# Adding the experts' output bias in TensorE's sum instead of in two passes over the tile

## The chip, the cores and the metric

The kernel runs on one core of one Trainium2 chip. The metric is device time in microseconds (us) of one execution, the median of several runs, lower is better. The engines are named as in the profile: PE is TensorE (PEld its weight loads), DVE is VectorE, ACT is ScalarE, POOL is GpSimd, SP is SyncE, which here only issues DMAs.

## The reference

The input is x, 16 sequences of 256 tokens with 128 channels: 4096 tokens. A RWKV block (layer norms, time shift, the wkv recurrence, a squared-ReLU channel mix) is followed by a residual sum and a layer norm. Then comes the part that the change touches, a mixture of 12 experts of which each token uses two:

```python
ys = _geglu(xf @ Ws1 + bs1) @ Ws2 + bs2                  # shared expert
logits = (xf @ Wr + br) / TAU
top_val, top_idx = jax.lax.top_k(logits, 2)
top_w = jax.nn.softmax(top_val, axis=-1)
w = jnp.einsum('nke,nk->ne', jax.nn.one_hot(top_idx, E), top_w)
h = jnp.einsum('nd,edh->enh', xf, We1) + be1[:, None, :]  # 128 -> 2 * 384
act = _geglu(h)
yE = jnp.einsum('enh,ehd->end', act, We2) + be2[:, None, :]
yr = jnp.einsum('end,ne->nd', yE, w)
out = layernorm(x + ys + yr)
```

The bias be2 (12 experts x 128 channels) is added to each expert's result, and the sum is weighed with the token's weight w.

## The kernel before

The first part (up to about 240 us) runs the RWKV block over eight chunks of 512 tokens, each engine following an order of steps that is written out by hand. It also routes: for every token and choice it computes a row in a table in HBM, `dispatched_rows`, in which each expert owns a region. POOL writes the rows there with 64 indirect DMAs (L403). From about 238 us SP places padding rows behind each expert's tokens (L1080, L1081: one register load and one DMA for each of 12 experts). The shared expert's matmuls (L1012, L1018, L1029) end at about 277 us.

The expert part then goes through 75 tiles (`TILES`) of 128 rows, each of one expert. What an engine does for tile n:

- **SP** copies the expert's first weights within SBUF into one of five buffers (`load_weights`, L1095, 384 KB), which waits until the up matmuls of tile n - 5 are done, and then loads the rows of tile n + 5 (`load_rows`, L1088, 68 KB) into one of ten buffers. Each needs a register load first (L1091, L1083). The two are issued in turn, in one queue.
- **PE** multiplies gate and up (`gate_of`, `up_of`, L1250: 3 + 3 matmuls of 128x128 in fp32, each shown as two records), transposes the rows of tile n + 2 (`turn_x`, L1242: one record), and then multiplies the second layer of tile n - 1 into one PSUM bank (`second`, L1268: 3 matmuls, 6 records).
- **ACT** applies Gelu to the gate (`gelu_of`, L1203, 3 operations), copies the transposed rows out of PSUM (`take_x`, L1197), and scales the expert's output bias by each row's weight into `wb` (`weigh_bias`, L1214). `be2_all` holds all 1536 bias values on each of the 128 partitions; SP loads it with one broadcast DMA (L1076), once the buffers that it overlays are free. The expert's number comes from a packed word that ACT loads into a register once for five tiles (`owners_of`).
- **DVE** multiplies up and gate (`act_of`, L1158, 3 operations), and then forms `yo = y * weight + wb` for the tile before (`give_y`, L1166). For every fifth tile it reads where the rows of the next five go (`where_to`, L1143 to L1150), which needs their rows loaded.
- **POOL** scatters `yo` to `routed_rows` in HBM with an indirect DMA (L1126).

Behind the last tile, SP waits for the scatters, loads both contributions back, PE sums them in PSUM, and a layer norm ends the kernel.

`ones_bf` is a 128x128 tile of ones in bf16 that the routing uses already (L387: the ones as stationary operand, in a chain of bf16 matmuls with 12 to 108 columns).

Of the kernel before, what the change touches and what calls it, by code (L numbers as in the profile page):

```python
# [14 lines left out]
def build(nc, x, out, vecs, rows, sqw, wfk, wfv, wrt, ws1, ws2, we1, we2, be1, be2, bs2):  # L15
    F32, BF16 = mybir.dt.float32, mybir.dt.bfloat16
    I32, U32 = mybir.dt.int32, mybir.dt.uint32
    ALU = mybir.AluOpType
# [44 lines left out]
    with ctx:  # L63
# [29 lines left out]
        bs2_col = sb("bs2_col", [P, C // P])  # L93
# [64 lines left out]
        z1 = tmp("z1", [P, CT, C])  # L158
        hT = tmp("hT", [P, SQ, T + 1])
# [7 lines left out]
        nmr3 = tmp("nmr3", [P, CT])  # L167
        pp = tmp("pp", [P, SQ, T + 1])
# [25 lines left out]
        be2_all = sb("be2_all", [P, E * C])  # L194
        after_hT = sb("after_hT", [P, SQ, T + 1])
# [33 lines left out]
        wb = [sb(f"wb{m}", [P, C]) for m in range(2)]  # L229
# [27 lines left out]
        for n in ("bias_spread wb_ready rows_known pads_placed tiles_known tiles_step "  # L257
# [23 lines left out]

        fin = [banks[c][:, :].rearrange("p (n c) -> p n c", c=C) for c in range(CH)]
# [5 lines left out]
        def attention_sync(sp):  # L288
# [15 lines left out]
            sp.dma_start(bs2_col[:, :], bs2.rearrange("(p a) -> p a", a=C // P)).then_inc(s["bias_loaded"], 16)  # L304
# [103 lines left out]
        def attention_vector(v):  # L408
# [57 lines left out]

            def stats(n, tiles, c):
# [120 lines left out]

            done = [0]
# [15 lines left out]
            def shared_take(c):  # L605
                if c == 0:
                    v.wait_ge(s["bias_loaded"], 16)
                v.wait_ge(s2["sh_out"], c + 1)
                at = slice(c * W, (c + 1) * W)
                nv.scalar_tensor_tensor(xnT_all[:, at], sh_y[c][:, :], bs2_col[:, 0:1], xnT_all[:, at], ALU.add, ALU.add).then_inc(s2["sh_taken"], 1)  # L610
# [49 lines left out]
            placed(v, 0, pT[:, PT_PREFIX]); one_over(5); output(5); weigh_v(6); stats2(5)  # L660
# [3 lines left out]
            stats2(7); chosen(v, 2); shared_act(0, 1); x3(6); mix(7); stats3(6)  # L664
# [407 lines left out]
        def experts_sync(sp):  # L1072

            sp.wait_ge(s["hT_psum"], CH)
            sp.wait_ge(s["x0_ready"], CH)
            sp.dma_start(be2_all[:, :], be2.rearrange("e c -> (e c)").partition_broadcast(P)).then_inc(s2["bias_spread"], 16)  # L1076
# [56 lines left out]
        def experts_vector(v):  # L1133
# [27 lines left out]
            def give_y(n):  # L1161
                after2(v, scattered[n % YO], n // YO * 16)
                v.wait_ge(s2["goes_ready"], n // U + 1)
                v.wait_ge(s2["wb_ready"], n + 1)
                v.wait_ge(s2["y_ready"], n + 1)
                nv.scalar_tensor_tensor(yo[n % YO][:, :], ps_y[:, 0:C], goes[n // U % DB][:, n % U, 1:2], wb[n % 2][:, :],  # L1166
                                        ALU.mult, ALU.add).then_inc(s2["yo_ready"], 1)
# [22 lines left out]
        def experts_scalar(a):  # L1190
# [15 lines left out]
            def owners_of(r):  # L1206

                packed_word = a.value_load(packed[0:1, ds(r, 1)])
                return [a.snap((packed_word >> (BITS * (m + 1))) & (2 ** BITS - 1)).with_bounds(min_val=0, max_val=E - 1) for m in range(U)]
# [6 lines left out]
            a.wait_ge(s2["owner_ready"], 1)  # L1216
            take_x(0)
            take_x(1)
            a.wait_ge(s2["bias_spread"], 16)
            for n in range(TILES):  # L1220
                if n % U == 0:
                    e = owners_of(n // U)
                gelu_of(n)
                if n + 2 < TILES:
                    take_x(n + 2)
                weigh_bias(n, e[n % U])
# [9 lines left out]
        def experts_tensor(t):  # L1236
            nt = nc.tensor

# [137 lines left out]
```

## Time and profile before

| | us |
|---|---|
| median of 3 runs | 486.0 |
| lowest and highest | 485.25, 486.16 |
| the profiled execution, whole | 485.25 |
| its span in the trace | 483.5 |

The profiled execution is the fastest of the three. Its span is 1.75 us shorter than its own time; what lies around the span isn't in the trace. Over the span PE is busy 83%, DVE 65%, ACT 62% and POOL 53%, but these are averages over a first part in which the engines take turns at being last, a stretch around 250 us in which PE, DVE and ACT stand nearly still, and the expert part from 277 to 452 us, which is 36% of the span. A time in a row is us from the start of the span, a mean is in ns.

### The profile page before, as it was taken

How to read it: one execution, taken by the hardware profiler on the slowest of the kernel's cores; microseconds unless marked ns; L12 is line 12 of the kernel's file. 1: busy time of each engine (PE TensorE's matmuls, PEld its weight loads, DVE VectorE, ACT ScalarE, POOL GpSimd, SP SyncE). 2: the span in 40 equal slices, each digit the busy share in tenths (PEclk: the TensorE clock that was granted, in tenths of full speed). 3: DMA queues.
4: the chain of work that ended last, by engine and by line, in shares of the span. 5: the costliest groups of instructions: out<-in, count | busy, mean ns of one | idle time of the engine just before them, and what ended most of it. 6: DMA issues, size and time to landing. Idle time of an engine off the chain costs nothing.

```text
span 483.5 us, 10004 instructions
## 1 busy us (share of the span) xinstructions
PE 403.4 (83%) x2503; PEld 307.7 (64%) x2503; DVE 314.1 (65%) x1065; ACT 297.9 (62%) x715; POOL 256.9 (53%) x328
## 2 busy tenths in 40 slices
PE   0276898998987979989464999999999999999992
PEld 0134456756746556664221489999999999999840
DVE  4769899999997996734521446665555655555252
ACT  2476699989785956754101167776666766666145
POOL 3657657567478867877472014444433443444264
PEclk9997899999999998999795989999999999999997
DMA  5399600000002001011121546766666666665294
GB/s 148 87 206 385 186 1 0 2 1 1 2 12 105 32 12 42 32 44 47 40 76 47 192 141 232 246 233 225 242 237 223 224 229 242 228 221 198 82 335 127
DMA packets 51471, 64.86 MB, mean 134 GB/s; under 512 B 8924, under 2 KB 35292, under 8 KB 51416
## 3 DMA queue, kind: packets, MB, share of 16 engines
q1 hardware_dynamic: 46968, 54.85, 34.3%
q0 software_dynamic: 4448, 9.38, 5.9%
q8 instruction: 22, 0.36, 0.3%
q14 instruction: 33, 0.27, 0.2%
HBM read 21.65 MB, written 13.91 MB: 74 GB/s over the span
## 4 chain that ended last, share of the span: by engine, by line
PE 46%; DVE 21%; issue 12%; SPq 8%; DMA 3%; POOL 3%; ACT 3%; another core or an unknown queue 2%; DVEq 0%; ACTq 0%; POOLq 0%
PE bank L1250 18%; PE bank L1268 9%; PE bank L981 4%; PE bank L963 3%; DVE bst L471 2%; SPq L1081 2%; DVE rec L551 2%; POOL frs L816 2%; SPq L1080 2%; PE bank L1018 1%; SPq L1095 1%; PE bank L1242 1%; PE bank L993 1%; DVE pp L507 1%
## 5 line engine op out<-in xcount | busy, mean ns | idle before, releaser
L1126 POOL DMA_INDIRECT routed_rows<-yo,goes_to x75 | 72.0, 959 | 123.8 <-DVE yo L1166 120.9
L1250 PE MATMUL bank<-xT,w 128*128 128x128 f32 x900 | 117.3, 280 | 3.5 <-issue 1.2
L1250 PEld LDWEIGHTS bank<-xT,w 128*128 128x128 f32 x900 | 108.9, 194 | 6.2 <-issue 3.6
L1158 DVE SCALAR_TENSOR_TENSOR actT<-bank,tile_bias,gl 128x128 f32<-128x128 f32 x225 | 65.6, 345 | 26.3 <-ACT gl L1203 13.2
L1203 ACT ACTIVATE gl<-bank,tile_bias 128x128 f32<-128x128 f32 x225 | 66.5, 365 | 24.2 <-PE bank L1250 23.5
L403 POOL DMA_INDIRECT dispatched_rows<-rows_all,slot_i x64 | 64.2, 1003 | 23.5 <-issue 17.3
L1268 PE MATMUL bank<-we_sb,actT 128*128 x450 | 63.8, 278 | 1.6 <-DVE yo L1166 1.1
L1268 PEld LDWEIGHTS bank<-we_sb,actT 128*128 128x128 f32 x450 | 56.1, 191 | 4.0 <-issue 3.6
L1166 DVE SCALAR_TENSOR_TENSOR yo<-bank,goes,wb 128x128 f32<-128x128 f32 x75 | 26.2, 350 | 34.2 <-PE bank L1268 28.2
L1197 ACT ACTIVATE xT<-bank 128x128 f32<-128x128 f32 x75 | 20.8, 278 | 32.2 <-PE bank L1242 22.9
L963 PE MATMUL bank<-xk,wfk_sb 128*128 128x512 f32 x64 | 32.5, 617 | 4.1 <-DVE xk L568 3.0
L602 DVE SCALAR_TENSOR_TENSOR below_m<-bank,v_sb,below_p 128x512 f32<-128x512 f32 x16 | 12.0, 748 | 36.0 <-remote 20.4
L914 PE MATMUL bank<-hT,mixa 128*128 128x512 f32 x48 | 28.6, 681 | 6.9 <-ACT hT L714 6.1
L776 ACT ACTIVATE below_p<-bank,v_sb 128x512 f32<-128x512 f32 x16 | 11.0, 687 | 37.7 <-remote 17.5
L981 PEld LDWEIGHTS bank<-wfv_sb,kf 128*128 128x128 f32 x256 | 29.4, 192 | 3.6 <-ACT kf L771 2.9
L981 PE MATMUL bank<-wfv_sb,kf 128*128 128x128 f32 x256 | 30.4, 277 | 0.8 <-ACT kf L771 0.8
L1214 ACT ACTIVATE wb<-be_all,goes 128x128 f32 x75 | 30.1, 402 | 1.2 <-issue 0.8
L900 PE MATMUL bank<-ident,z 128*128 128x128 f32 x64 | 10.6, 291 | 22.8 <-ACT z L685 22.8
L844 POOL TENSOR_TENSOR rstd<-veps,half 128x4 f32<-128x4 f32 x24 | 27.8, 1156 | 1.9
L1029 PE MATMUL bank<-below_m,ws_sb 128*128 128x512 f32 x32 | 19.1, 727 | 9.9 <-DVE below_m L602 9.8
L551 DVE RECIPROCAL rec<-nd 128x512 f32<-128x512 f32 x8 | 26.7, 3341 | 0.1
L915 PE MATMUL bank<-hT,mixb 128*128 128x512 f32 x48 | 26.7, 640 | 0.0
(201 smaller groups left out, 772.8 us busy)
## 6 DMA issues: line engine op xcount, KB each, us to landing
w<-we_sb SPq DMA_DIRECT2D x75, 384.0 KB
x_all<-dispatched_rows SPq DMA_DIRECT2D x75, 68.0 KB
we_sb<-we SPq DMA_DIRECT2D x1, 4608.0 KB
rows_all<-x SPq DMA_DIRECT2D x8, 256.0 KB, 2.7
x_all<-routed_rows SPq DMA_DIRECT2D x8, 256.0 KB, 4.9
rows_all<-routed_rows SPq DMA_DIRECT2D x8, 256.0 KB, 5.1
out<-x_all SPq DMA_DIRECT2D x8, 256.0 KB, 2.5
routed_rows<-yo,goes_to POOLq DMA_INDIRECT x75
```

What stands on the lines that cost most here:

```text
L403: ng.indirect_dma_start(dispatch, bass.IndirectOffsetOnAxis(ap=slot_i[:, k, n:n + 1], axis=0), rows_all[:, n, :], None).then_inc(s["dispat ...
L551: nv.reciprocal(rec[:, :], nd[:, 1, :]).then_inc(s["rec_ready"], 1)
L844: ng.tensor_tensor(rstd[n][:, :], veps[n][:, :], half[:, :], ALU.pow).then_inc(s["pow" + n], 1)
L914: nt.matmul(o, mixa[:, n, :], hT[:, :, 1:T + 1], start=True, stop=False)
L963: nt.matmul(pf[j % 2][:, :], wfk_sb[:, j * P:(j + 1) * P], xk2[:, :], start=True, stop=True).then_inc(s["fk_ready"], 1)
L981: last = nt.matmul(pkv[:, n * P:(n + 1) * P], kf[:, j, n * P:(n + 1) * P], wfv_sb[:, j, :], start=j == 0, stop=j == HF - 1)
L1126: ng.indirect_dma_start(routed, bass.IndirectOffsetOnAxis(ap=goes_to[n // U % DB][:, n % U:n % U + 1], axis=0), yo[n % YO][:, :], None).th ...
L1158: nv.scalar_tensor_tensor(actT[n % UA][:, at], ps_a[j][:, 0:P], tile_bias[:, j, n:n + 1], gl[n % 2][:, at], ALU.add, ALU.mult).then_inc(s2 ...
L1203: na.activation(gl[n % 2][:, j * P:(j + 1) * P], ps_g[j][:, 0:P], ACT.Gelu, bias=tile_bias[:, HK + j, n:n + 1]).then_inc(s2["gelu_ready"], 1)
L1214: na.activation(wb[n % 2][:, :], be2_all[:, ds(e * C, C)], ACT.Copy, scale=goes[n // U % DB][:, n % U, 1:2]).then_inc(s2["wb_ready"], 1)
L1250: return nt.matmul(to[:, 0:P], w1[m][:, off:off + P], xT[m][:, :], start=True, stop=True)
L1268: last = nt.matmul(ps_y[:, 0:C], actT[m][:, j * P:(j + 1) * P], we2_sb[:, ds(e, 1), j, :].rearrange("p a c -> p (a c)"), start=j == 0, sto ...
```

## The change

The bias is no longer scaled by ACT and added by DVE. PE adds it while the tile's second layer is still being summed in PSUM, so that DVE only multiplies by the weight: `(y + b) * w` in place of `y * w + b * w`.

For this the bias is split into three bf16 parts whose sum is the fp32 value (`split_biases`, five small DVE operations on 128x13 elements, placed behind `output(5)`). The parts are moved by three small DMAs into partitions 0, 1 and 2 of a new tile `bias_rows` (bf16, 128 x 1536), whose other partitions are zero (`zero_bias_rows`, a memset placed ahead of `stats2(7)`). A matmul with `ones_bf` as stationary operand sums the partitions and so puts the bias on every row of the tile (`biased`).

What goes: ACT's operation, its register load and its waits; the wait of DVE on `wb_ready`; the broadcast DMA of 768 KB and SP's waits ahead of it. What comes: one bf16 matmul for each tile, the five operations and the memset on DVE, one more small load and the three DMAs on SP, and a wait of PE for these ahead of the tiles. The buffers `z1` and `hT` change places with some small ones, so that `bias_rows` overlays `z0` and `z0w`.

```diff
+        braw = sb("braw", [P, NB])
+        bpart = [sb(f"bpart{n}", [P, NB], BF16) for n in range(3)]
...
-        be2_all = sb("be2_all", [P, E * C])
-        after_hT = sb("after_hT", [P, SQ, T + 1])
+        bias_rows = sb("bias_rows", [P, E * C], BF16)
...
-            sp.dma_start(bs2_col[:, :], bs2.rearrange("(p a) -> p a", a=C // P)).then_inc(s["bias_loaded"], 16)
+            sp.dma_start(braw[:, 0:B2], be2.rearrange("e h -> (e h)").rearrange("(p a) -> p a", a=B2)).then_inc(s["bias_loaded"], 16)
+            sp.dma_start(braw[:, B2:NB], bs2.rearrange("(p a) -> p a", a=NB - B2)).then_inc(s["bias_loaded"], 16)
...
+            def split_biases():
+                v.wait_ge(s["bias_loaded"], 2 * 16)
+                for n, (of, to) in enumerate(((braw, bleft), (bleft, bleft2))):
+                    nv.tensor_copy(bpart[n][:, :], of[:, :]).then_inc(s["split"], 1)
+                    v.wait_ge(s["split"], 2 * n + 1)
+                    nv.tensor_tensor(to[:, :], of[:, :], bpart[n][:, :], ALU.subtract).then_inc(s["split"], 1)
+                    v.wait_ge(s["split"], 2 * n + 2)
+                nv.tensor_copy(bpart[2][:, :], bleft2[:, :]).then_inc(s["split"], 1)
...
+            def zero_bias_rows():
+                nv.memset(bias_rows[:, :], 0.0).then_inc(s["rows_zero"], 1)
...
-            placed(v, 0, pT[:, PT_PREFIX]); one_over(5); output(5); weigh_v(6); stats2(5)
+            placed(v, 0, pT[:, PT_PREFIX]); one_over(5); output(5); split_biases(); weigh_v(6); stats2(5)
...
-            stats2(7); chosen(v, 2); shared_act(0, 1); x3(6); mix(7); stats3(6)
+            zero_bias_rows(); stats2(7); chosen(v, 2); shared_act(0, 1); x3(6); mix(7); stats3(6)
...
-            sp.wait_ge(s["hT_psum"], CH)
-            sp.wait_ge(s["x0_ready"], CH)
-            sp.dma_start(be2_all[:, :], be2.rearrange("e c -> (e c)").partition_broadcast(P)).then_inc(s2["bias_spread"], 16)
+            sp.wait_ge(s["rows_zero"], 1)
+            sp.wait_ge(s["split"], 5)
+            for n in range(3):
+                sp.dma_start(bias_rows[n:n + 1, :], bpart[n][:, 0:B2]).then_inc(s2["rows_moved"], 16)
...
-                v.wait_ge(s2["wb_ready"], n + 1)
                 v.wait_ge(s2["y_ready"], n + 1)
-                nv.scalar_tensor_tensor(yo[n % YO][:, :], ps_y[:, 0:C], goes[n // U % DB][:, n % U, 1:2], wb[n % 2][:, :],
-                                        ALU.mult, ALU.add).then_inc(s2["yo_ready"], 1)
+                nv.tensor_scalar(yo[n % YO][:, :], ps_y[:, 0:C], goes[n // U % DB][:, n % U, 1:2], None, ALU.mult).then_inc(s2["yo_ready"], 1)
...
-            def weigh_bias(n, e):
-                a.wait_ge(s2["goes_ready"], n // U + 1)
-                after2(a, "yo_ready", n - 1)
-                na.activation(wb[n % 2][:, :], be2_all[:, ds(e * C, C)], ACT.Copy, scale=goes[n // U % DB][:, n % U, 1:2]).then_inc(s2["wb_ready"], 1)
...
+            def biased(to, row, width):
+
+                return nt.matmul(to, ones_bf[:, :], bias_rows[:, ds(row, width)], start=False, stop=True)
...
-                    last = nt.matmul(ps_y[:, 0:C], actT[m][:, j * P:(j + 1) * P],
-                              we2_sb[:, ds(e, 1), j, :].rearrange("p a c -> p (a c)"), start=j == 0, stop=j == HK - 1)
-                last.then_inc(s2["y_ready"], 1)
+                    nt.matmul(ps_y[:, 0:C], actT[m][:, j * P:(j + 1) * P],
+                              we2_sb[:, ds(e, 1), j, :].rearrange("p a c -> p (a c)"), start=j == 0, stop=False)
+                biased(ps_y[:, 0:C], e * C, C).then_inc(s2["y_ready"], 1)
...
+            t.wait_ge(s2["rows_moved"], 3 * 16)
```

How the instructions stand in a row is shown at two places. First PE in the middle of the expert part, from the last up matmul of one tile to the first gate matmul of the next (bank6 is the last up bank, bank7 the bank of the second layer, bank0 the first of the gate). Before:

```order
L1250 MATMUL bank6<-xT2,w1_2 128x128 [waits e_act_ready]
L1242 MATMUL bank4<-ident,x0_all 128x128 [waits e_xT_ready,x_loaded2_9]
L1268 REGISTER_ALU [waits e_yo_ready,e_act_ready]
...
L1268 ISA
L1268 MATMUL bank7<-we2_sb,actT1 128x128
L1250 MATMUL bank0<-xT3,w1_3 128x128 [waits e_gelu_ready,w1_loaded3,e_xT_ready]
```

And with the change:

```order
L1255 MATMUL bank6<-xT2,w1_2 128x128 [waits e_act_ready]
L1247 MATMUL bank4<-ident,x0_all 128x128 [waits e_xT_ready,x_loaded2_9]
L1273 REGISTER_ALU [waits e_yo_ready,e_act_ready]
...
L1273 ISA
L1273 MATMUL bank7<-we2_sb,actT1 128x128
L1242 ISA
L1242 MATMUL bank7<-bias_rows,ones_bf 128x128
L1255 MATMUL bank0<-xT3,w1_3 128x128 [waits e_gelu_ready,w1_loaded3,e_xT_ready]
```

The bf16 matmul and one register instruction stand between the last fp32 matmul of the second layer and the next gate.

The second place is ACT at the start of the expert part (gl is the Gelu's result, xT the transposed rows). Before:

```order
L1197 ACTIVATE xT0<-bank4 128x128 [waits e_xT_psum,e_owner_ready,e_bias_ready]
L1197 ACTIVATE xT1<-bank4 128x128 [waits e_xT_psum]
L1208 TENSOR_LOAD packed [waits e_bias_spread]
L1203 ACTIVATE gl0<-bank0,tile_bias 128x128 [waits e_gate_ready]
...
L1197 ACTIVATE xT2<-bank4 128x128 [waits e_xT_psum]
L1214 REGISTER_ALU [waits e_goes_ready]
...
L1214 ACTIVATE wb0<-be2_all,goes0 128x128
L1203 ACTIVATE gl1<-bank0,tile_bias 128x128 [waits e_gate_ready]
```

With the change:

```order
L1213 ACTIVATE xT0<-bank4 128x128 [waits e_xT_psum,e_bias_ready]
L1213 ACTIVATE xT1<-bank4 128x128 [waits e_xT_psum]
L1219 ACTIVATE gl0<-bank0,tile_bias 128x128 [waits e_gate_ready]
...
L1213 ACTIVATE xT2<-bank4 128x128 [waits e_xT_psum]
L1219 ACTIVATE gl1<-bank0,tile_bias 128x128 [waits e_gate_ready]
```

The register load, two register instructions, the move of an address and the scaling are gone between the copy of one tile's rows and the Gelu of the next tile.

## Rows read from the trace of the kernel before

**Rows 1.** Busy time by stretch: us, then PE, PEld, DVE, ACT, POOL, PEclk, DMA share, GB/s.

```profile
277.00:452.00 175.00, 168.18 (x1425) 162.87 (x1426) 99.99 (x360) 116.55 (x375) 70.93 (x74) 0.99 0.63 217
```

**Rows 2.** Page, part 5: groups of instructions of the expert part.

```profile
L1250 PE MATMUL bank<-xT,w 128*128 128x128 f32 x900 | 117.3, 280 | 3.5 <-issue 1.2
...
L1166 DVE SCALAR_TENSOR_TENSOR yo<-bank,goes,wb 128x128 f32<-128x128 f32 x75 | 26.2, 350 | 34.2 <-PE bank L1268 28.2
...
L1214 ACT ACTIVATE wb<-be_all,goes 128x128 f32 x75 | 30.1, 402 | 1.2 <-issue 0.8
```

**Rows 3.** Timeline of PE: start us, us, engine line operation; transpositions mark the tiles.

```profile
284.15 0.27 PE L1242 MATMUL bank<-ident,x_all 128*128 128x128 f32 x1
...
291.28 1.57 PE L1250 MATMUL bank<-xT,w 128*128 128x128 f32 x12
...
373.33 0.27 PE L1242 MATMUL bank<-ident,x_all 128*128 128x128 f32 x1
...
375.45 0.27 PE L1242 MATMUL bank<-ident,x_all 128*128 128x128 f32 x1
...
439.57 1.58 PE L1250 MATMUL bank<-xT,w 128*128 128x128 f32 x12
...
445.22 0.27 PE L1242 MATMUL bank<-ident,x_all 128*128 128x128 f32 x1
```

**Rows 4.** Timeline of SP's queue: weight copies of tiles 5, 20 and 70, and a row load.

```profile
284.66 0.50 SPq L1095 DMA_DIRECT2D w<-we_sb  x1
...
318.83 0.49 SPq L1095 DMA_DIRECT2D w<-we_sb  x1
319.90 0.34 SPq L1088 DMA_DIRECT2D x_all<-dispatched_rows  x1
...
434.93 0.49 SPq L1095 DMA_DIRECT2D w<-we_sb  x1
```

**Rows 5.** Chain that ended last, 374 to 396 us: start us, us, what.

```profile
373.93 0.49 SPq L1095
...
376.14 0.49 SPq L1095
...
377.21 0.71 SPq L1088
...
387.89 4.16 DMA w<-we_sb
...
392.14 1.58 PE bank L1250 x12
```

**Rows 6.** Timeline of POOL in the same stretch.

```profile
377.17 0.96 POOL L1126 DMA_INDIRECT routed_rows<-yo,goes_to  x1 [1.16 <-DVE yo L1166]
```

**Rows 7.** Timelines of PE and PEld: fp32 matmuls with 12 columns, and bf16 ones.

```profile
214.79 1.05 PE L951 MATMUL bank<-wrt_sb,xnT_all 128*128 128x12 f32 x8 [1.50 <-issue]
...
227.52 1.02 PE L1012 MATMUL bank<-xnT_all,ws_sb 128*128 128x512 f32 x2
...
228.43 0.39 PE L387 MATMUL bank<-sel,ones_bf 128*128 128x96 bf16 x8
228.67 1.11 PE L1018 MATMUL bank<-xnT_all,ws_sb 128*128 128x512 f32 x2
...
228.38 0.34 PEld L387 LDWEIGHTS bank<-sel,ones_bf 128*128 128x128 bf16 x8 [0.18 <-issue]
```

**Rows 8.** Timeline of DVE where its new operations go, and two small operations.

```profile
149.11 0.87 DVE L471 BATCH_NORM_STATS2 bst<-x1c 128x6 f32<-128x128 f32 x4 [2.51 <-ACT x1c L751]
...
192.59 0.87 DVE L471 BATCH_NORM_STATS2 bst<-x1c 128x6 f32<-128x128 f32 x4 [4.08 <-ACT x1c L751]
...
238.73 0.17 DVE L620 TENSOR_TENSOR ntl<-run_f,base_tile 128x12 f32<-128x12 f32 x1
238.94 0.18 DVE L621 TENSOR_TENSOR_SCAN edge_of<-ones_ex,ntl 128x13 f32<-128x13 f32 x1
```

**Rows 9.** Waits of SP's queue: us in total, times, longest.

```profile
SPq L1080 <- DVE wait_here L617: 88.3, 1, 88.3
```

More of the change, by code:

```diff
@@ L92, in build @@
         LN1W, LN1B, LN2W, LN2B, DECAY, FIRST, TMK, TMV, TMR, CMK, CMR, BS1 = range(12)
-        bs2_col = sb("bs2_col", [P, C // P])
+        NB = (E * C + C) // P
+        braw = sb("braw", [P, NB])
+        bleft = sb("bleft", [P, NB])
+        bleft2 = sb("bleft2", [P, NB])
+        bpart = [sb(f"bpart{n}", [P, NB], BF16) for n in range(3)]
+        B2 = E * C // P
         be1_sb = sb("be1_sb", [E, H1])
@@ L157, in build @@
         z0w = tmp("z0w", [P, CT, C])
-        z1 = tmp("z1", [P, CT, C])
-        hT = tmp("hT", [P, SQ, T + 1])
         bst = {n: tmp(f"bst{n}", [P, CT, 6]) for n in "0123"}
@@ L167, in build @@
         nmr3 = tmp("nmr3", [P, CT])
+        z1 = tmp("z1", [P, CT, C])
+        hT = tmp("hT", [P, SQ, T + 1])
         pp = tmp("pp", [P, SQ, T + 1])
@@ L228, in build @@
         yo = [sb(f"yo{m}", [P, C]) for m in range(YO)]
-        wb = [sb(f"wb{m}", [P, C]) for m in range(2)]
         w1 = [sb(f"w1_{m}", [P, H1]) for m in range(U)]
@@ L256, in build @@
         s2 = {}
-        for n in ("bias_spread wb_ready rows_known pads_placed tiles_known tiles_step "
+        for n in ("rows_moved rows_known pads_placed tiles_known tiles_step "
                   "word_psum code_psum code_ready bias_psum bias_ready owner_ready own_ready goes_step goes_ready "
@@ L280, in gate_bank @@
             return pkv if j and c >= EARLY else pv
+        bs2_col = braw[:, B2:NB]
         fin = [banks[c][:, :].rearrange("p (n c) -> p n c", c=C) for c in range(CH)]
@@ L606, in shared_take @@
                 if c == 0:
-                    v.wait_ge(s["bias_loaded"], 16)
+                    v.wait_ge(s["bias_loaded"], 2 * 16)
                 v.wait_ge(s2["sh_out"], c + 1)
                 at = slice(c * W, (c + 1) * W)
-                nv.scalar_tensor_tensor(xnT_all[:, at], sh_y[c][:, :], bs2_col[:, 0:1], xnT_all[:, at], ALU.add, ALU.add).then_inc(s2["sh_taken"], 1)
+                nv.scalar_tensor_tensor(xnT_all[:, at], sh_y[c][:, :], bs2_col, xnT_all[:, at], ALU.add, ALU.add).then_inc(s2["sh_taken"], 1)
             def find_tiles():
@@ L1204, in gelu_of @@
                                   bias=tile_bias[:, HK + j, n:n + 1]).then_inc(s2["gelu_ready"], 1)
-            def owners_of(r):
-                packed_word = a.value_load(packed[0:1, ds(r, 1)])
-                return [a.snap((packed_word >> (BITS * (m + 1))) & (2 ** BITS - 1)).with_bounds(min_val=0, max_val=E - 1) for m in range(U)]
-            def weigh_bias(n, e):
-                a.wait_ge(s2["goes_ready"], n // U + 1)
-                after2(a, "yo_ready", n - 1)
-                na.activation(wb[n % 2][:, :], be2_all[:, ds(e * C, C)], ACT.Copy, scale=goes[n // U % DB][:, n % U, 1:2]).then_inc(s2["wb_ready"], 1)
-            a.wait_ge(s2["owner_ready"], 1)
             take_x(0)
             take_x(1)
-            a.wait_ge(s2["bias_spread"], 16)
             for n in range(TILES):
-                if n % U == 0:
-                    e = owners_of(n // U)
                 gelu_of(n)
@@ L1225, in experts_scalar @@
                     take_x(n + 2)
-                weigh_bias(n, e[n % U])
             for c in range(CH):
```

## The prediction

> **What bounds the kernel now.** I read the windows first, to see which part the change touches: the expert part, 277 to 452 us, in which PE is busy 168.2 of 175.0 us at a granted clock of 0.99, ACT 116.6 and DVE 100.0 [rows 1]. That looks like a PE bound. The timeline of PE says how tight it is. In a tile without a stall one transposition follows the last after 2.12 us (373.33 to 375.45) [rows 3], and a tile is 12 records of gate and up (900 over 75 tiles) [rows 2], 6 of the second layer and the transposition: 19 records, so 0.1116 us each. From the transposition at 284.15 to that at 445.22 there are 71 tiles in 161.07 us [rows 3], where 71 x 2.12 would be 150.5. So 10.5 us of the part are stalls, and something else than PE limits it as well.
>
> That something is SP's queue. Its weight copies for tiles 5 and 20 are issued 34.17 us apart, 2.278 each, and those for tiles 20 and 70 116.1 us apart, 2.322 each; over all 65 it is 2.312 [rows 4]. In the chain of waits SP's instructions follow one another without a wait: from copy to copy 2.21 us in the best case (373.93 to 376.14) [rows 5]. It is slower than a clean PE tile, so PE eats up its lead. The copy of tile 5 is issued 6.62 us ahead of its matmuls (284.66, 291.28), that of tile 70 only 4.64 us (434.93, 439.57) [rows 3, 4]; and it can't be much less, since a copy takes 4.16 us to land and the gate starts 0.09 us behind it (387.89, 392.14) [rows 5]. The lead of 6.62 - 4.25 = 2.37 us is used up after 2.37 / (2.278 - 2.12) = 15 tiles, about tile 20. From there PE waits for SP.
>
> **The change, part by part.**
>
> *The bf16 matmul, 75 times.* What a record costs here is the load of its weights, not its columns: eight fp32 records with 12 columns take 1.05 us [rows 7], of which the last one's own duration is some 0.28 [rows 2], so (1.05 - 0.28) / 7 = 0.110 us each, as much as with 128 columns. A bf16 load is short: eight in 0.34 us, at most 0.043 each [rows 7]. But the next fp32 load begins only when the bf16 matmul starts and can't hide behind an fp32 matmul any more: the two fp32 matmuls behind a bf16 one span 1.11 us where two behind an fp32 one span 1.02 [rows 7], 0.09 more. So a bf16 matmul ahead of an fp32 load costs nearly one full record. Bounds: 0.05 us (0.39 / 8, the bf16 matmuls with up to 96 columns [rows 7]) and 0.112 (a record). I take 0.107, nearest to the 0.09 and the 0.112. PE's tile becomes 2.227 us and its sum grows by 75 x 0.107 = 8.0 us. The register instruction ahead of it runs in the sequencer, as the three of the fp32 matmuls do in tiles without a stall: nothing.
>
> The Trainium skill, "TensorE: Matmul & The Clock Gate", section "Back-to-back issue gap", gives about 81 ns for a sustained pair of load and matmul with 128 columns; by it the sum would be 6.1 us. Its section "LDWEIGHTS (loading the stationary operand)" gives columns / 1.2, so 107 ns for 128, which agrees with the 0.112 here.
>
> *What ACT loses.* 75 x 0.402 = 30.1 us of work [rows 2], with a register load in every fifth tile. ACT is busy 116.6 of 175 us and doesn't bound a tile [rows 1]: nothing.
>
> *What DVE loses.* The wait for `wb`; the multiplication stays, of 0.350 us, and waited mostly for PE's second layer (28.2 of 34.2 us) [rows 2]. Between 0 and the rest that wasn't PE's, 6 us; DVE too is far from full [rows 1], so 0.
>
> *The end of the expert part.* It is the later of two times for the start of tile 70's matmuls, 439.57 before [rows 3].
> - By PE: it starts tile 5 at 291.28, later by the four bf16 matmuls until then, 0.43. Without stalls tile 70 starts at 291.71 + 65 x 2.227 = 436.5.
> - By SP: the copy of tile 5 goes out at 284.66, unchanged. Copy 70 follows 65 intervals later, and the matmuls 4.64 us behind it. At 2.278, the rate of the stretch in which PE doesn't stall: 284.66 + 148.1 + 4.64 = 437.4. At 2.322, the rate of the later stretch: 440.2. At 2.21, the best case: 432.9, so PE decides.
>
> Which rate? SP is slowed where POOL's indirect DMA, 0.96 us from 377.17, falls on SP's row DMA: that took 0.71 us from 377.21, where one took 0.34 away from it [rows 4 to 6]. PE's tile sets POOL's beat. In the late stretch, where PE waits for SP, both beats lock with POOL's on top of SP's. A PE at 2.227 is as slow as an SP at about 2.26 and stays out of this longer, as in the first 15 intervals. So I take 2.278 and 437.4, 2.2 us ahead of 439.57. Behind it come six bf16 matmuls (those of tiles 69 to 74), 0.64. Sum: -1.5 us, with bounds -2.5 (PE decides: 436.5 - 439.57 + 0.64) and +1.3 (2.322). At the low price of 0.05 PE's own end only moves ahead, and SP's stays: the price hardly matters.
>
> *The first part.* The five small operations on DVE: one follows the other after 0.21 us [rows 8], 1.05 us together. They go ahead of the states of chunk 6, behind which DVE waits 2.51 us for ACT [rows 8]: hidden; without that cover +1.05. The memset goes where DVE waits 4.08 us for ACT [rows 8], hidden; no row has its size, and I bound it by a 128x512 operation, 0.87 us [rows 8]. SP's three small DMAs wait for that memset, at about 190 us, and stand ahead of the padding, for which SP sits waiting 88.3 us [rows 9]: nothing, or 3 x 0.5 us if they came late. The broadcast that goes was issued into the same wait: between 0 and -0.5.
>
> **The sum.** 485.25 - 1.5 = 483.7 for an execution like the profiled one. The median of the runs lies 0.75 above it: **484.5**.
>
> **The rivals.**
> - *SP keeps its whole mean of 2.312.* Its end for tile 70 is then that of before, and only the six last matmuls are added: +0.6, 486.6. For it: 50 of 65 intervals ran at 2.322 [rows 4]. Against: they ran in the lock that a slower PE avoids.
> - *The stalls aren't SP's but belong to the group of five tiles.* DVE reads where rows go for each five, and PE waits behind DVE. If such a stall has a fixed size, a slower PE doesn't absorb it, and the price comes in full: 75 x 0.107 = +8.0, 494. It decides if the leads of copies at the stalls are well above 4.25 us. Against: at tile 70 the lead is 4.64, and the first 15 tiles hardly stall though they have the same groups. In between, half of the stalls being fixed gives about +3, 489.
> - *The first part moves.* The five operations or SP's DMAs aren't hidden: up to +1.05 and +1.5, 487 to 488 if the end stays.
> - *PE decides alone* (SP at 2.26 or less): -2.5, 483.5; with less at the start and a cheaper bf16 matmul, 482.5.
>
> **How the numbers follow.** 0.2% is 1 us, about what a measurement of this kernel can tell from no change. My forecast with the PE-bound case beside it: 45%. SP as before, or the forecast with a small loss in the first part: 30%. Fixed stalls in full 12%, in part or a loss in the first part 13%. Faster 0.45, same 0.30, slower 0.25. The forecast's own range is 482.7 to 485.6. The range that should hold 8 in 10 reaches to 490 and leaves out the full price (12%) and some 6% below 482.3.
>
> **What would show it.** In the profile of the changed kernel a tile without a stall should take 2.23 us (2.17 if the bf16 matmul costs only its columns). The bf16 group should have 75 records, and the gate behind each start 0.11 us later. From the fourth transposition to the last, 71 tiles should take 159 to 161 us and the stalls 1 to 3 us in place of 10.5. Copies 5 and 70 should be 148 us apart (150.3 before). ACT should lose 30 us of busy time. The first row load and the first tile should stand where they do, within 1 us. I'm wrong if SP's intervals stay at 2.31, if stalls stay at 10 us beside longer tiles, or if the expert part starts later.

## The result, and the profile after

The changed kernel takes 488.75 us (median of 13 runs, 486.58 to 492.09), the kernel before 486.0 in the same rounds. The medians are 2.75 us apart, where I had forecast 1.5 us faster. The ratio is 1.0082, 95% interval 1.0059 to 1.0104, which is 4.0 us and more than the medians say: it is that of the means of all 38 executions of the changed kernel on record (489.64) and of the 13 of the kernel before (485.62). So the loss here is 2.75 to 4.0 us. Of all executions below, one is left out of the numbers: one of e16's six, which took 1410.45 us. The profiled execution of the changed kernel took 491.54 us, with a span of 489.8; before it was 485.25 and 483.5. So the two profiled executions are 6.3 us apart where the medians are 2.75 apart, and a difference between these two traces alone isn't the price of the change. I come back to that below with more executions.

Busy time of the expert part, 4 us later than in [rows 1] since everything begins later (columns as there), and what the page groups there, to be held against [rows 2]:

```profile
281.00:456.00 175.00, 171.88 (x1492) 168.05 (x1493) 98.91 (x358) 87.67 (x300) 70.10 (x73) 0.98 0.62 216
```

```profile
L1255 PE MATMUL bank<-xT,w 128*128 128x128 f32 x900 | 119.5, 283 | 1.4 <-DVE actT L1176 0.5
...
L1183 DVE TENSOR_SCALAR yo<-bank,goes 128x128 f32<-128x128 f32 x75 | 26.3, 350 | 38.9 <-PE bank L1242 36.5
```

ACT has gone from 116.6 to 87.7 us: its scaling is away, nearly the 30.1 us that it had. DVE's `give_y` still takes 350 ns and still waits, now for the bf16 matmul (L1242). PE is fuller, 171.9 of 175 for 168.2. The view of line L1242 alone shows the new work, one line for each kind of instruction with its shortest, middle and longest duration in ns:

```profile
L1242 PEldq FUSED_REGOPS  x75: 46/46/46, 288.0 to 457.4; - x75
L1242 PEld LDWEIGHTS bank<-bias_rows,ones_bf x75: 100/100/100, 289.3 to 457.8; 128*128 128x128 bf16 x75
L1242 PE MATMUL bank<-bias_rows,ones_bf x75: 219/219/219, 289.4 to 457.9; 128*128 x75
```

The durations overlap with their neighbours, so the price is read from starts. PE's timeline, answering to [rows 3]:

```profile
288.62 0.27 PE L1247 MATMUL bank<-ident,x_all 128*128 128x128 f32 x1
290.85 0.27 PE L1247 MATMUL bank<-ident,x_all 128*128 128x128 f32 x1
...
295.31 0.27 PE L1247 MATMUL bank<-ident,x_all 128*128 128x128 f32 x1
295.42 0.83 PE L1273 MATMUL bank<-we_sb,actT 128*128 x6
296.09 0.22 PE L1242 MATMUL bank<-bias_rows,ones_bf 128*128 x1
296.14 1.56 PE L1255 MATMUL bank<-xT,w 128*128 128x128 f32 x12
297.54 0.27 PE L1247 MATMUL bank<-ident,x_all 128*128 128x128 f32 x1
...
450.99 0.27 PE L1247 MATMUL bank<-ident,x_all 128*128 128x128 f32 x1
```

A tile without a stall takes 2.23 us (288.62 to 290.85, 295.31 to 297.54) where it took 2.12: the bf16 matmul costs 0.11 (0.109 with three digits, 2.228 less 2.119), though the next gate starts only 0.05 behind it. From the fourth transposition to the last there are 71 tiles in 162.37 us, 161.07 before. The longer tiles make 71 x 0.11 = 7.8 us of that; the stalls fell from 10.5 to 4.0. SP's queue, answering to [rows 4] (the copies of tiles 5, 20 and 70; the last row holds two copies):

```profile
288.77 0.52 SPq L1113 DMA_DIRECT2D w<-we_sb  x1
...
323.81 0.49 SPq L1113 DMA_DIRECT2D w<-we_sb  x1
...
440.38 1.50 SPq L1113 DMA_DIRECT2D w<-we_sb  x2
```

151.61 us for the 65 intervals, 2.332 each, where it was 2.312. The chain of waits runs through SP as it did in [rows 5], one instruction behind the other from copy to copy (L1109 and L1101 are the register loads):

```profile
291.01 0.49 SPq L1113
291.54 0.27 SPq L1101
291.89 0.07 SPq L1106
292.08 0.34 SPq L1106
292.46 0.52 SPq L1109
293.20 0.49 SPq L1113
```

Of these 2.19 us, 0.83 are the two DMA issues (0.49 and 0.34), and 0.79 are the two register loads (0.27 and 0.52).

In the first part the new operations stand where they were put. DVE's timeline at the two places of [rows 8], and SP's waits, where [rows 9] had one of 88.3 us:

```profile
146.23 0.17 DVE L475 CAST bpart<-braw 128x13 bf16<-128x13 f32 x1
146.44 0.17 DVE L477 TENSOR_TENSOR bleft<-braw,bpart 128x13 f32<-128x13 f32 x1
...
150.09 0.87 DVE L485 BATCH_NORM_STATS2 bst<-x1c 128x6 f32<-128x128 f32 x4 [1.56 <-ACT x1c L768]
...
190.88 0.70 DVE L604 MEMSET bias_rows<- 128x768 uint32 x1
194.65 0.88 DVE L485 BATCH_NORM_STATS2 bst<-x1c 128x6 f32<-128x128 f32 x4 [3.07 <-ACT x1c L768]
```

```profile
SPq L1098 <- DVE wait_here L634: 48.6, 1, 48.6
SPq L1094 <- DVE bias_rows L604: 44.3, 1, 44.3
```

The five operations follow each other after 0.21 us, as estimated, and the wait behind them is 1.56 for 2.51 us; the memset takes 0.70 and the wait is 3.07 for 4.08. The covers took both. On SP the memset now holds the three small DMAs until it is done, 44.3 us, which fell into the wait that was there before. Yet the first transposition of the expert part starts at 281.84, where it was 277.88: 4 us that no new instruction accounts for. The chain of waits has pieces that it gives to no engine and no known queue. In the kernel before, from 226 to 236 us:

```profile
228.66 2.88 another core or an unknown queue
...
231.71 3.36 another core or an unknown queue
```

and in the changed one, from 205 to 235 us:

```profile
213.13 5.92 another core or an unknown queue
...
230.59 2.33 another core or an unknown queue
```

### The profile page after: what moved, and what is told of

Read it like the earlier page. It is cut to its first block, busy times and chain, and to the rows that moved or that the text cites. A ratio compares the mean times of both kernels' runs of the same rounds, so it can differ in the third digit from the quotient of the medians.

```text
span 489.8 us, 9786 instructions
## 1 busy us (share of the span) xinstructions
PE 409.8 (84%) x2578; PEld 315.6 (64%) x2578; DVE 314.8 (64%) x1071; ACT 268.6 (55%) x640; POOL 256.4 (52%) x328
## 4 chain that ended last, share of the span: by engine, by line
PE 34%; SPq 22%; DVE 16%; issue 13%; ACT 5%; DMA 3%; POOL 3%; another core or an unknown queue 2%; ACTq 0%; DVEq 0%; POOLq 0%
PE bank L1255 9%; SPq L1113 6%; SPq L1106 5%; PE bank L1273 4%; SPq L1109 4%; PE bank L980 4%; PE bank L998 3%; SPq L1101 3%; SPq L1098 2%; SPq L1099 2%; PE bank L931 2%; DVE bst L485 2%; PE bank L932 2%; PE bank L1010 1%
## 5 line engine op out<-in xcount | busy, mean ns | idle before, releaser
L1255 PE MATMUL bank<-xT,w 128*128 128x128 f32 x900 | 119.5, 283 | 1.4 <-DVE actT L1176 0.5
L1183 DVE TENSOR_SCALAR yo<-bank,goes 128x128 f32<-128x128 f32 x75 | 26.3, 350 | 38.9 <-PE bank L1242 36.5
L980 PE MATMUL bank<-xk,wfk_sb 128*128 128x512 f32 x64 | 35.0, 657 | 4.7 <-DVE xk L582 3.0
L931 PE MATMUL bank<-hT,mixa 128*128 128x512 f32 x48 | 27.4, 654 | 8.3 <-ACT hT L731 7.5
L998 PE MATMUL bank<-wfv_sb,kf 128*128 128x128 f32 x256 | 30.1, 276 | 0.5 <-ACT kf L788 0.5
L1247 PE MATMUL bank<-ident,x_all 128*128 128x128 f32 x75 | 21.0, 280 | 7.8 <-DMA x_all<-dispatched_rows 7.8
L917 PEld LDWEIGHTS bank<-ident,z 128*128 128x128 f32 x64 | 8.2, 154 | 29.4 <-issue 23.6
```

The source lines that it names most:

```text
L931: nt.matmul(o, mixa[:, n, :], hT[:, :, 1:T + 1], start=True, stop=False)
L980: nt.matmul(pf[j % 2][:, :], wfk_sb[:, j * P:(j + 1) * P], xk2[:, :], start=True, stop=True).then_inc(s["fk_ready"], 1)
L998: last = nt.matmul(pkv[:, n * P:(n + 1) * P], kf[:, j, n * P:(n + 1) * P], wfv_sb[:, j, :], start=j == 0, stop=j == HF - 1)
L1255: return nt.matmul(to[:, 0:P], w1[m][:, off:off + P], xT[m][:, :], start=True, stop=True)
```

## The experiments

18 kernels ran, in five groups, each group on one chip, each kernel in five rounds against the kernel before. In three of these groups (e1 to e4, e9 to e12, e17 and e18) the kernel before takes 462 us, in the two others (e5 to e8, e13 to e16) 487. I call them the groups at 462 and at 487; the two profiles above, of 485.25 and 491.54 us, are of the kind at 487. What makes the difference isn't known, and that it is the chip isn't shown: the record gives the same chip number, 10, for e13 to e16 (487) and for e17 and e18 (462).

The difference lies ahead of the expert part. In the groups at 462 the first transposition stands near 255 us and the chain of waits has no piece of unknown origin. The largest single part of it is SP's placing of the padding rows. It takes 29.3 to 30.5 us in every profile at 487, and 15.1 to 15.6 in every one at 462, with and without the change. First the kernel before (487), then e12 (462), the same twelve DMAs (shortest, middle and longest in ns, first and last start in us):

```profile
L1081 SPq DMA_DIRECT2D dispatched_rows<-pad_rows x12: 5/510/725, 239.4 to 268.9; - x12
```

```profile
L1083 SPq DMA_DIRECT2D dispatched_rows<-pad_rows x12: 496/516/657, 229.3 to 244.1; - x12
```

The expert part takes nearly the same time in both kinds (about 1 us more at 487). So a kernel is compared only with the kernel before in its own group.

For each kernel I give the ratio with its 95% interval, and from its profile "71 tiles" (fourth to last transposition) with the stalls in them (what they take beyond the clean tile's time), and SP's mean interval from copy 5 to copy 70.

### Is it the matmul, or what was taken away? (e1 to e3)

**e1**: the kernel before without the weighed bias. be2 is left out of the result here, and in e2, e11, e14, e17 and e18.

```diff
-            sp.dma_start(be2_all[:, :], be2.rearrange("e c -> (e c)").partition_broadcast(P)).then_inc(s2["bias_spread"], 16)
...
-                nv.scalar_tensor_tensor(yo[n % YO][:, :], ps_y[:, 0:C], goes[n // U % DB][:, n % U, 1:2], wb[n % 2][:, :],
-                                        ALU.mult, ALU.add).then_inc(s2["yo_ready"], 1)
+                nv.tensor_scalar(yo[n % YO][:, :], ps_y[:, 0:C], goes[n // U % DB][:, n % U, 1:2], None, ALU.mult).then_inc(s2["yo_ready"], 1)
...
-                weigh_bias(n, e[n % U])
```

> The kernel before without the weighed bias: ACT's operation, its register loads, DVE's wait and the broadcast DMA of 768 KB are gone, and be2 is left out of the result. Theory A (SP's queue limits the expert part; what the change takes from ACT and DVE is worth nothing): no change, -0.5 to +0.5 us against before. Rival (ACT's relief is worth something): -2 us or more, all of it in the expert part.

Measured: 462.51 for 462.15 us, 1.0005 (0.9993 to 1.0017). 71 tiles 161.45, stalls 10.9, SP 2.314. Taking 30 us of work from ACT and a wait from DVE gives nothing.

**e2**: the change without its matmul.

```diff
-                    nt.matmul(ps_y[:, 0:C], actT[m][:, j * P:(j + 1) * P],
-                              we2_sb[:, ds(e, 1), j, :].rearrange("p a c -> p (a c)"), start=j == 0, stop=False)
-                biased(ps_y[:, 0:C], e * C, C).then_inc(s2["y_ready"], 1)
+                    last = nt.matmul(ps_y[:, 0:C], actT[m][:, j * P:(j + 1) * P],
+                              we2_sb[:, ds(e, 1), j, :].rearrange("p a c -> p (a c)"), start=j == 0, stop=j == HK - 1)
+                last.then_inc(s2["y_ready"], 1)
```

> The changed kernel without the bf16 matmul (be2 is left out of the result): it differs from e1_no_wb by the additions in the first part alone (five small DVE operations, the memset, one small load, three small DMAs of SP, the order of buffers). Theory A (the loss sits ahead of the expert part and comes from these additions): +2.5 to +4 us against before, the first expert tile 3 to 4 us later. Rival B (the first part's waits for an unknown queue only vary from run to run; the loss is the bf16 matmul's): -0.5 to +1 us against before.

Measured: 462.24 us, 0.9997 (0.998 to 1.0013). 71 tiles 159.99, stalls 9.5, SP 2.300. Without the matmul nothing of the loss is left in this group, so the first part isn't it here.

**e3**: the kernel before with a bf16 matmul of zeros behind each second layer.

```diff
+            nv.memset(zero_bf[:, :], 0.0)
...
-                last.then_inc(s2["y_ready"], 1)
+                nt.matmul(ps_y[:, 0:C], ones_bf[:, :], zero_bf[:, :], start=False, stop=True).then_inc(s2["y_ready"], 1)
```

> The kernel before with one more bf16 matmul for each tile (ones by a tile of zeros, into the same sum; nothing else is changed). Theory A (SP's queue limits the part, so a longer PE tile is mostly hidden): +0.5 to +1.5 us, a tile without a stall 2.23 us in place of 2.12. Rival (the price is seen in full): +8 us. Rival B (the whole loss is the matmul's): +4 us.

Measured: 464.64 us, 1.0053 (1.0034 to 1.0073): +2.5. 71 tiles 160.92, stalls 2.6, SP 2.294. The matmul alone makes a loss of this size, with ACT's and DVE's old work still in place. It is more than my theory's +0.5 to +1.5 and less than the rival's +4.

### Is SP's queue the limit? (e4, e16)

**e4** and **e16**: the kernel before, where SP keeps the expert's number of tile n in a register from its row load to its weight copy, instead of loading the word a second time. The DMAs and their order are the same.

```diff
             def load_rows(n):
                 at = sp.value_load(word[0:1, n:n + 1])
+                if n >= U:
+                    owner_kept[n] = sp.snap(at & 15).with_bounds(min_val=0, max_val=E - 1)
...
             def load_weights(n):
-                at = sp.value_load(word[0:1, n:n + 1])
-                e = sp.snap(at & 15).with_bounds(min_val=0, max_val=E - 1)
+                e = owner_kept.pop(n) if n >= U else sp.snap(sp.value_load(word[0:1, n:n + 1]) & 15).with_bounds(min_val=0, max_val=E - 1)
```

> The kernel before with one register load less for each tile on SP: the word of tile n, read for its rows, is kept for its weight copy. Theory A (SP's instructions, 2.31 us for each tile, limit the expert part): SP's interval falls to about 1.95 us where it isn't held, PE's tiles run at 2.12 without stalls, the 71 tiles take 151 us in place of 161, and the time falls by 8 to 10 us. Rival (the stalls come from the DMAs' landing times or from DVE's work for each five tiles): no change within 1 us.

> The kernel of e4 (before with one register load less for each tile on SP): -9 to -11 us on any chip, 71 tiles in 150.5 to 151 us, since PE's tile and SP's interval are the same on the chips seen.

Measured: e4 452.17 for 462.15 us, 0.9772 (0.9754 to 0.9791); e16, in a group at 486.83, 477.65, 0.981 (0.9775 to 0.9846), so -9.2 us. The windows of e4 over its expert part, columns as in [rows 1]:

```profile
261.00:411.00 150.00, 150.00 (x1346) 149.99 (x1345) 93.76 (x339) 110.38 (x355) 66.80 (x70) 1.00 0.70 247
```

PE has no idle time at all. 71 tiles take 150.64 us, which is 71 x 2.12, and the stalls are 0.1 us. e16's profile has 151.39 us, so 0.9 of stalls, a little more than expected. SP's copies follow each other as PE frees the buffers:

```profile
329.91 0.49 SPq L1098 DMA_DIRECT2D w<-we_sb  x1
331.05 0.34 SPq L1092 DMA_DIRECT2D x_all<-dispatched_rows  x1
332.03 0.49 SPq L1098 DMA_DIRECT2D w<-we_sb  x1
```

One register load less in each of 70 tiles takes 10 us off in e4 and 9.2 in e16. That shows that SP's queue limits the kernel before, and that its 10.5 us of stalls are SP's. At the start of the part, where SP is still ahead of PE's buffers, its first three intervals are 1.64 to 1.68 us in e4, where the same queue needed 2.21 at best with both loads. It is also a version that beats both kernels, without the change.

### What does the matmul cost where nothing covers it? (e7, e8)

**e7**: the change with e4's edit. **e8**: e3 (the matmul of zeros) with e4's edit. **e5** and **e6** are the changed kernel and the kernel before once more, in the same group (486.73 us).

> The changed kernel, unaltered, beside the kernel before on the chip of this call. e3 showed that the matmul alone costs 2.5 us, and e1 and e2 that all the rest of the change costs nothing on their chip. Theory A' (the loss is the matmul's, and the first part of the change is free): +2 to +3 us. Rival (the first part of the change costs on top): +4 us or more.

> The kernel before, unaltered, as if it were another: no change, within 0.5 us. Its profile gives the start of the expert part and the 71 tiles for this chip: 71 tiles in 160.5 to 161.5 us.

> The changed kernel with one register load less for each tile on SP. Theory A (with SP out of the way PE decides, and the bf16 matmul is seen in full): 71 tiles in 158.3 us (2.23 each, no stalls), so 3 us less than before, and 8 us more than the kernel before with the same edit (e4: 150.6 us for the 71 tiles). Rival (the matmul costs what it cost in e3, 2.5 us, whatever limits the part): 71 tiles in 153 us.

> The kernel before with one register load less on SP and with the bf16 matmul of zeros, nothing else changed. Theory A: as e7_after_one_load within 1 us, so about 2 us faster than before, since the rest of the change (relief of ACT and DVE, first part) is worth nothing. Rival (ACT's relief counts once PE decides): slower than e7 by 2 us or more.

| | us | ratio | 71 tiles | stalls | SP |
|---|---|---|---|---|---|
| e5 | 489.26 | 1.0049 (1.0022 to 1.0075) | 161.92 | 3.6 | 2.335 |
| e6 | 486.44 | 1.0012 (0.9989 to 1.0035) | 159.94 | 9.4 | 2.306 |
| e7 | 487.11 | 1.0006 (0.9981 to 1.0031) | 158.84 | 0.5 | 2.206 |
| e8 | 485.93 | 0.999 (0.9966 to 1.0014) | 158.75 | 0.4 | 2.204 |

PE's timeline of e7, two transpositions near the start of the part and the last two:

```profile
285.78 0.27 PE L1250 MATMUL bank<-ident,x_all 128*128 128x128 f32 x1
288.00 0.27 PE L1250 MATMUL bank<-ident,x_all 128*128 128x128 f32 x1
...
440.17 0.27 PE L1250 MATMUL bank<-ident,x_all 128*128 128x128 f32 x1
442.39 0.27 PE L1250 MATMUL bank<-ident,x_all 128*128 128x128 f32 x1
```

With SP out of the way PE alone sets the pace in both: 158.8 against the 150.6 of e4, 8.2 us for 71 matmuls, 0.115 each (0.105 against e16, which is of a group at 487 as e7 is). This is the price in full, and here it eats the whole gain of e4: e7 and e8 stand where the kernel before stands. In the changed kernel as it is, SP's slowness hides most of it.

The tiles came out as expected, the times didn't: I had expected 3 us less for e7 and 2 less for e8, and the medians are at +0.4 and -0.8. From the first transposition to the end of the span e7 and e8 take 203.5 and 203.8 us, 2.1 to 2.4 less than e6 (205.9). By that 1.3 to 2.8 us are lost ahead of the tiles in the timed executions, and where is open. The profiles can't tell: that of e7 is an execution of 482.52 us, 4.6 below its own median. e6's 71 tiles are 0.6 us under what I expected too.

### What is left of it in the kernel as it is? (e9 to e12)

In one group at 462.03 us: **e9** the changed kernel, **e10** e3 again, **e11** e2 again, and **e12** the kernel before with 75 bf16 matmuls behind PE's last sum, where no one waits for them. e12 asks whether a longer program of PE costs something by itself.

```diff
+            t.wait_ge(s2["fin_out"], 1)
+            for n in range(TILES):
+                nt.matmul(banks[0][:, 0:C], ones_bf[:, :], zero_bf[:, :], start=True, stop=True)
```

> The changed kernel unaltered, as the measure for the three beside it on this chip. From e5: +2 to +4 us against before. In the profile 71 tiles in 161 to 162.5 us, 1 to 2 more than before.

> The kernel of e3 (before with the bf16 matmul of zeros alone) beside the changed one on the same chip. Theory A' (the whole loss is the matmul's): as e9 within 0.7 us. Rival C (the additions in the first part cost 1 to 2 us where the chip is slow, as e7 against e8 hints): 1 to 2 us less than e9.

> The kernel of e2 (the change without its matmul, be2 left out) on this chip. Theory A': within 0.7 us of before, as in e2. Rival C: +1 to +2 us.

> The kernel before with 75 bf16 matmuls of zeros placed behind PE's last sum, where PE has nothing to do until the end, so that its program is as long as with the change and no tile is. Rival D (a longer program of PE costs time in the first part, through instruction fetches): +1 to +2 us. Theory A' (the loss is the tiles' own): within 0.5 us of before.

| | us | ratio | 71 tiles | stalls | SP |
|---|---|---|---|---|---|
| e9 | 464.43 | 1.0043 (1.0026 to 1.006) | 160.18 | 1.8 | 2.308 |
| e10 | 463.96 | 1.0039 (1.0019 to 1.0059) | 160.47 | 2.1 | 2.304 |
| e11 | 462.4 | 1.0013 (0.9998 to 1.0028) | 159.58 | 9.1 | 2.302 |
| e12 | 461.74 | 0.9991 (0.9976 to 1.0006) | 159.09 | 8.6 | 2.294 |

The matmul is again the loss (+1.9 alone, +2.4 with everything), and not by the length of the program as such: e12 has as many, placed behind the tiles, and costs nothing. e9's 71 tiles are under the 161 to 162.5 that I expected. e12's last row of PE also gives the price of bf16 matmuls in a row. The row's 4.35 us hold the last one's own 0.22, so they start (4.35 - 0.22) / 74 = 0.056 us apart, half of what one costs between fp32 matmuls:

```profile
450.36 4.35 PE L1318 MATMUL bank<-zero_bf,ones_bf 128*128 128x128 bf16 x75
```

### Does the first part cost something of its own? (e13 to e15, e17, e18)

In a group at 486.83 us: **e13** the changed kernel, **e14** without the matmul (as e2), **e15** the matmul of zeros alone (as e3). Then, to tell a cost of the additions from scatter between programs, **e17** (as e1) and **e18** (as e2) in one group.

> The changed kernel unaltered, as the measure for e14 and e15: +2 to +4 us against before.

> The kernel of e2 (the change without its matmul, be2 left out). Theory A' (the first part of the change is free): within 0.7 us of before on any chip. Rival C (it costs where the chip is slow): +1 to +2 us if the kernel before takes 486 us here.

> The kernel of e3 (before with the matmul of zeros alone). Theory A': as e13 within 0.7 us. Rival C: 1 to 2 us less than e13 if the kernel before takes 486 us here.

> The kernel before without the weighed bias, as e1: ACT's scaling, its register loads, the wait of DVE and the broadcast are gone, nothing is added (be2 is left out of the result). Theory: the additions of the change to the first part cost something on a chip where the kernel before takes 486 us, and the removals nothing: ratio within 0.998 and 1.002, no different from the kernel before. Rival: the scatter between programs on such a chip is itself 0.5%, so that any changed program can stand at 1.005 to 1.006 there: then this kernel too may lie outside 0.998 to 1.002. On a chip where the kernel before takes 462 us both expect 0.999 to 1.001.

> The change without its matmul, as e2, e11 and e14 (be2 is left out of the result): the split, the memset, the three DMAs and the new places of the buffers stay. Theory, that these cost 2.8 us on a chip where the kernel before takes 486 us: ratio 1.004 to 1.008 there, and 1.000 to 1.001 on a chip where it takes 462 us. Rival, that the 2.8 us of e14 were scatter: ratio within 0.998 and 1.003 on the former too.

| | us | before | ratio | 71 tiles | stalls | SP |
|---|---|---|---|---|---|---|
| e13 | 489.22 | 486.83 | 1.0068 (1.0042 to 1.0094) | 162.38 | 4.0 | 2.328 |
| e14 | 489.6 | 486.83 | 1.0062 (1.003 to 1.0094) | 160.97 | 10.4 | 2.299 |
| e15 | 488.55 | 486.83 | 1.0034 (1.0006 to 1.0063) | 160.89 | 2.6 | 2.303 |
| e17 | 463.13 | 462.1 | 1.0008 (0.9991 to 1.0026) | 159.16 | 8.6 | 2.290 |
| e18 | 461.71 | 462.1 | 0.9999 (0.9987 to 1.0012) | 159.27 | 8.7 | 2.278 |

e14 is at +2.8 us with no matmul in it, which neither the theory (0.7 at most) nor the rival (1 to 2) allowed. That speaks for a cost of the first part in a group at 487. But it doesn't add up with the others: the matmul alone gives +1.7 (e15), and both together (e13) give +2.4, no more than e14 by itself. In the pair e7 and e8, which differ by the first part and by ACT's and DVE's relief, it is 1.2 us. e17 and e18 came to a group at 462, where e18 repeats e2: nothing. They so left the question open for which they were made. In such groups the first part costs -0.4 to 0.5 us (e18, e2, e11, e9 less e10), and in those at 487 between 0.7 (e13 less e15) and 2.8 (e14), which isn't settled.

One difference between the two kinds bears on it. At 462 the chain to the first transposition runs through POOL's row DMAs, the last of which ends at 249.4 to 251.4 us, when SP has long placed the padding (243.3 to 245.7). At 487 it is the other way round: POOL's end at 258.1 to 263.7 and the padding at 268.8 to 275.4, and the chain runs through the padding, which starts when DVE has the row numbers. So a delay of DVE there has no cover behind it at 487. That this is what e14 shows is argued, not shown.

Nor is it known what makes the waits of unknown origin: they are 8.1 us in the chain of the kernel before (four pieces), 12.3 in that of e6 (three), 10.9 in that of the changed kernel (three), and in the groups at 462 there are none in the chain. They come without the change too, at other places each time, so it is not shown that the change adds to them.

## Why the prediction was wrong, point by point

All profiles together, to take some of the scatter out: nine profiles without the matmul (the kernel before, e1, e2, e6, e11, e12, e14, e17, e18), seven with it (the changed kernel, e3, e5, e9, e10, e13, e15).

| means, us | without | with |
|---|---|---|
| 71 tiles | 160.1 (159.1 to 161.5) | 161.3 (160.2 to 162.4) |
| stalls in them | 9.5 | 3.0 |
| SP's interval, copy 5 to 70 | 2.300 | 2.315 |
| from the issue of copy 70 to the last transposition | 10.3 | 10.8 |
| first transposition to the end of the span | 205.2 | 206.9 |

Most of the profiles with the whole change are of groups at 487, and most of those without the matmul of groups at 462, so two of these rows are also given apart (number of profiles in brackets):

| means, us | without | matmul alone | whole change |
|---|---|---|---|
| SP's interval, groups at 487 | 2.306 (3) | 2.303 (1) | 2.332 (3) |
| SP's interval, groups at 462 | 2.296 (6) | 2.299 (2) | 2.308 (1) |
| first transposition to the end, at 487 | 205.9 | 206.4 | 207.7 |
| first transposition to the end, at 462 | 204.8 | 206.2 | 206.0 |

- **The price of the bf16 matmul** was right: 0.107 taken, 0.11 measured in a clean tile, 0.105 to 0.115 in e7 against e16 and e4. The reason that I gave, that the fp32 load behind it can't be hidden, agrees with e12, where bf16 matmuls in a row cost 0.056, but no run tests it by itself. One reading in it was wrong: a bf16 load isn't 0.043 us short. The eight loads of [rows 7] take 96 to 99 ns each and overlap, so that 0.043 says only how closely they follow each other. In the changed kernel the load takes 100 ns. The Trainium skill, "TensorE: Matmul & The Clock Gate", section "LDWEIGHTS (loading the stationary operand)", gives columns / 1.2, so 107 ns for 128 columns. The trace's 100 ns is near that. For a sustained pair of load and matmul with 128 columns the Trainium skill, on the same page, section "Back-to-back issue gap", gives about 81 ns. Neither number here agrees with it: one bf16 matmul between fp32 ones costs 0.109 us, and e12's 75 pairs in a row 0.056 each.
- **SP's queue as the limit** was right, and is shown by e4 and e16.
- **The relief of ACT and DVE at nothing** was right (e1, e17).
- **The absorption by stalls** was right in kind and nearly in size. I forecast 159 to 161 us for the 71 tiles and 1 to 3 us of stalls; the profile of the changed kernel has 162.4 and 4.0, the mean of the seven is 161.3 and 3.0. Of 7.8 us, 6.5 vanish in the stalls.
- **The step that failed is SP's rate.** I took 2.278, that of the first 15 intervals, for the whole part, and so -2.2 us for the matmuls of tile 70. I explained the 2.322 of the later ones by POOL's DMAs falling in step with SP's, out of which a slower PE would keep. The profiles don't show such an effect. With the matmul SP's mean is 2.294 to 2.335, and never lower than the lowest without (2.278). Nor does it matter whether POOL's DMA falls on SP's row DMA: in e12 the 47 intervals in which it does take 2.290 us in the mean, the 18 others 2.306; in the kernel before it is 2.331 and 2.261, but in the changed one 2.336 and 2.326. And the early stretch isn't a quicker one: over the nine profiles without the matmul the first 15 intervals are at 2.299 and the other 50 at 2.300, in e12 at 2.311 and 2.289. About four intervals in five are ordinary ones, 2.264 us in the kernel before and 2.268 in the changed one, and the others are long, 12 of mean 2.52 and 13 of mean 2.59. The kernel before had two of them in its first 15, as few as any of the nine, and I had built a mechanism on it. They aren't mere chance either, though POOL's beat isn't their reason: the intervals behind copies 23 and 37 are long (over 2.40 us) in all 16 profiles and that behind copy 51 in 14, so at these three the place in SP's program counts. What happens there is open. At SP's unchanged mean the term is 0 in place of -2.2.
- **The six last matmuls** (+0.64) were right: from the issue of copy 70 to the last transposition the time grows by 0.5.
- **What is then left** is my first rival, "SP keeps its whole mean", with +0.6, 486.6. Measured is more, by the medians +2.4 to +2.75 for the whole change in its four groups (by the ratios +2.0 to +4.0), and +1.7 to +2.5 for the matmul alone. Only a part of the rest can be placed. At 487 the whole change makes SP's interval longer, by 0.026 in the mean, 65 x 0.026 = 1.7 us; the matmul alone doesn't there (2.303), and at 462 the one profile of the whole change (2.308) lies within those without (2.278 to 2.314). Why the whole change slows SP at 487 is open. From the first transposition to the end of the span, which holds both SP's term and the last six matmuls, the whole change adds 1.8 us at 487 and 1.2 at 462, the matmul alone 0.5 and 1.4. What is lost ahead of the first transposition the profiles can't size: it stands at 277.3 to 283.8 us in the groups at 487 and at 254.4 to 256.4 in those at 462, with and without the first part of the change.
- **The first part**: the covers for the five operations, the memset and SP's DMAs held as worked out, and in the groups at 462 its cost was within what I allowed. That the first tile stands 4 us later in the profile after can be the scatter of single executions in large part: at 487 the five profiles with the first part have it at 280.4 in the mean (277.3 to 282.2), the five without at 279.5 (277.9 to 283.8). The rest is open, see e14.
- **Fixed stalls, in full**: refuted. In e4 the stalls are gone, so none were fixed.

The range held 488.75; the sign and the chances didn't. The mistake behind them is that I took a gain of 2.2 us from a difference of 0.044 us between two stretches of one execution, and gave the case without it only 30%. A matmul added to the engine next to the limit had no row that showed a gain from it; its sure terms were zero or positive, but for the broadcast's 0 to -0.5.

## What to carry to other kernels

Where one queue issues two DMAs for each tile, count its register loads too: here they were a third of its interval, and one of them less was worth 9 to 10 us, where 30 us taken from a busy engine off the path were worth nothing. Work that is added to the second slowest engine is hidden up to the limit's pace, but the start and the end of the pipeline still pay, and once the limit is lifted the full price comes back. A rate read from 15 intervals of one execution isn't a mechanism: see first whether a second execution has it. And a trace of one group stands only for its own kind: two means that mix groups at 462 and at 487 in different shares differ by that alone.

## What the runs showed of the hardware

- A bf16 matmul of 128 columns costs 0.11 us between fp32 ones (2.12 to 2.23 us for a clean tile) and 0.056 in a row of its kind (e12).
- A register load by SP takes 0.27 and 0.52 us in the chain of the changed kernel. To drop one in each tile brought SP's mean interval from 2.31 to 2.10 us (e4), where PE's pace was the limit; where it wasn't, from 2.21 to 1.64 to 1.68.
- The same kernel takes 462 us in some groups and 487 in others. The clean tile is 2.12 us in both. Ahead of the expert part the twelve padding DMAs of SP take 30 us in place of 15, and ACT and DVE wait for something that the profile has no name for. The mean granted clock of the profiled executions is lower as well, 0.944 to 0.957 in place of 0.962 to 0.978, which can be a result of the longer waits as well as a part of the reason; no run tells them apart. The waits without a name between 205 and 256 us, first of the kernel before, then of e12:

```profile
ACT below_p L776 <- remote: 12.4, 2, 10.9
DVE below_m L602 <- remote: 5.7, 2, 3.0
```

```profile
ACT xnT_all L732 <- remote: 3.2, 1, 3.2
```
